# A decoder layer on one core: the projections moved one step further ahead of the scores, with their transfers in another order

## What is computed

```python
q, k, v = (split_heads(x @ W.T + b) for each of the three)
scores = (q @ Wq_lsr) @ (k @ Wk_lsr).T / sqrt(32)
attn = softmax(where(causal, scores, -inf))
x = layernorm(x + (attn @ v) @ Wo.T + bo)
x = layernorm(x + cross_attention(x, ctx))      # 120 context rows, 8 heads' width
x = layernorm(x + ffn(x, x shifted by one token))
```

## Time and profile before

| | us |
|---|---|
| median of 3 runs (lowest, highest) | 1104.71 (1097.24, 1111.92) |
| the profiled execution, its time | 1103.24 |
| its span, first to last instruction | 1101.5 |
| TensorE busy, share of the span | 980.6, 89% |
| DVE busy | 809.7, 74% |
| ACT busy | 582.0, 53% |
| POOL busy | 285.3, 26% |

### The profile page before, as it was taken

One profiled execution on the slowest core, in us unless ns is written; L12 is line 12 of the kernel. 1 busy time (PEld: TensorE's weight loads), 2 busy tenths in 40 slices (PEclk: granted clock), 3 DMA queues, 4 the chain that ended last, 5 costly groups with the idle time before them and its releaser, 6 DMA issues.

```text
span 1101.5 us, 24092 instructions
## 1 busy us (share of the span) xinstructions
PE 980.6 (89%) x8740; PEld 761.0 (69%) x8804; DVE 809.7 (74%) x1725; ACT 582.0 (53%) x1121; POOL 285.3 (26%) x537
## 2 busy tenths in 40 slices
PE   4667899999999999999999999999999999998863
PEld 4446677777777777777776777777777777776652
DVE  5335788788788787878787878878888787876453
ACT  1123455556665555566565555666555555565532
POOL 5000122222233222223322222223322223222332
PEclk9678999999999998999999999999999999999886
DMA  7664565666565566664655566655655666660000
GB/s 178 117 109 102 110 112 105 126 131 125 114 121 102 112 111 103 131 126 107 119 112 109 108 106 131 131 116 119 111 114 120 108 103 128 131 122 25 21 11 19
DMA packets 114784, 118.57 MB, mean 108 GB/s; under 512 B 20649, under 2 KB 98283, under 8 KB 114667
## 3 DMA queue, kind: packets, MB, share of 16 engines
q1 hardware_dynamic: 114667, 117.03, 54.4%
HBM read 74.00 MB, written 41.94 MB: 105 GB/s over the span
## 4 chain that ended last, share of the span: by engine, by line
DMA 38%; PE 26%; SPq 16%; ACT 8%; issue 7%; POOL 2%; DVE 2%; ACTq 0%; POOLq 0%; DVEq 0%
DMA parts_dram<-parts 25%; SPq L358 12%; DMA stack<-parts_dram 12%; PE ps_m L482 5%; PE ps_m L474 3%; PE ps_t L500 3%; PE ps_s L500 3%; ACT sum L703 2%; PE ps_t L506 2%; ACT x L679 2%; PE ps_o L552 2%; ACT yT_hi L696 1%; SPq L329 1%; PE ps_s L506 1%; ACT parts L671 1%
## 5 line engine op out<-in xcount | busy, mean ns | idle before, releaser
L662 ACT ACTIVATE p<-ps_t 128x1024 f32<-128x1024 f32 x192 | 196.6, 1024 | 129.3 <-PE ps_t L506 110.5
L856 DVE TENSOR_REDUCE row_max<-ps_s 128x4 f32<-128x1024 f32 (+1 forms) x192 | 232.8, 1213 | 43.2 <-PE ps_s L506 28.5
L1054 POOL TENSOR_TENSOR var<-mv,eps 128x2 f32<-128x2 f32 x96 | 18.8, 196 | 602.0 <-DVE mv L879 602.0
L500 PE MATMUL ps_s<-stack 48*128 48x128 f32 (+1 forms) x1024 | 109.3, 313 | 46.4 <-DMA stack<-parts_dram 41.3
L500 PEld LDWEIGHTS ps_s<-stack 48*128 48x128 f32 x1024 | 73.7, 191 | 82.4 <-DMA stack<-parts_dram 46.4
L500 PEld LDWEIGHTS ps_t<-stack 50*128 50x128 f32 x1024 | 73.7, 191 | 61.9 <-issue 43.3
L500 PE MATMUL ps_t<-stack 50*128 50x128 f32 (+1 forms) x1024 | 109.5, 314 | 5.3 <-ACT p L662 3.2
L772 ACT COPY kxT<-ps_m 128x240 f32<-128x240 f32 x32 | 11.5, 358 | 189.7 <-PE ps_m L454 189.7
L552 PE MATMUL ps_o<-p,v_pad 128*32 128x256 f32 (+1 forms) x2048 | 96.3, 329 | 0.0
L552 PEld LDWEIGHTS ps_o<-p,v_pad 128*32 128x32 f32 x2048 | 57.5, 109 | 39.3 <-issue 17.4
L1080 POOL TENSOR_TENSOR xr_lo<-dx,xr_hi 128x512 fp32r<-128x512 f32 x32 | 40.8, 1274 | 141.9 <-ACT xr_hi L736 141.9
(11 more groups left out here) (167 smaller groups left out, 2801.8 us busy)
## 6 DMA issues: line engine op xcount, KB each, us to landing
stack<-parts_dram SPq DMA_DIRECT2D x384, 128.0 KB, 4.4
parts_dram<-parts SPq DMA_DIRECT2D x64, 512.0 KB, 5.3
x_in<-in_x_turned SPq DMA_DIRECT2D x32, 256.0 KB, 2.9
x_res<-in_x SPq DMA_DIRECT2D x32, 256.0 KB, 3.2
out_x<-sum SPq DMA_DIRECT2D x64, 128.0 KB, 1.8
ctxT<-in_ctx_turned SPq DMA_DIRECT2D x32, 120.0 KB, 5.6
stack<-shift_parts SPq DMA_DIRECT2D x128, 8.0 KB
p<-in_Wq SPq DMA_DIRECT2D x1, 256.0 KB, 2.8
```

The costliest lines, as they stand in the source:

```text
L500: nc.tensor.matmul(o, left[b.slot][r0:r0 + rows_n, h // 2, rows_at:rows_at + P], right[b.slot][r0:r0 + rows_n, h // 2, col:col + width], s ...
L662: nc.scalar.activation(p[c][:], ps_t[:], ACT.Exp).then_inc(exp_done[c], 1)
L856: nc.vector.tensor_reduce(row_max[:, tile, :, j0:j0 + nj], ps_s[:].rearrange("p (g j w) -> p g j w", j=nj, g=2), AX_X, ALU.max) \
```

## The change

The stage numbers become 0, 2, 3, 4, 5: IN runs two steps ahead of SCORES, and the other stages keep their distances. There is one step more in all. In SP's step, the parts of q and of k are each written as soon as they are there, x_in of the next batch follows the k parts, and the twelve stack loads stand last, behind the shift rows. Before it overwrites a slot in DRAM, SP waits for the loads from it of three batches ago. POOL sets the ones rows of slot 0 where it set all three before, and the other two after the constants; SP waits for a semaphore of the slot instead of `consts_ready`. The engines' `on` becomes a dictionary.

```diff
-IN, SCORES, PROBS, CROSS, FFN = range(5)
+IN, SCORES, PROBS, CROSS, FFN = 0, 2, 3, 4, 5
...
-            def load_x(b):
-                wait(sp, v_["xT_lo"], b.n)
-                sp.dma_start(x_in[:], tokens(x_turned, b.n).rearrange("(k p) t -> p k t", p=P)).then_inc(x_loaded, 16)
+            def save_parts(b, s, ready):
+
+                if b.n >= RING:
+                    sp.wait_ge(stack_loaded[b.slot], Batch(b.n - RING, IN).dma_count(12))
+                sp.wait_ge(v_[ready], b.n + 1)
+                sp.dma_start(parts_dram[s][b.slot].rearrange("(a p) w t -> p a w t", p=P), parts[s][:].bitcast(F32)) \
+                    .then_inc(parts_saved[s][b.slot], 16)
+
+            def load_stack(b, s, which):
+
+                sp.wait_ge(parts_saved[s][b.slot], b.dma_count(1))
+                for g in range(2):
+                    for row, part in enumerate(which):
...
 
             def step(at):
-
-                if live(at, IN) and at > 0:
-                    load_x(Batch(at, IN))
-                at = at - 1
                 b = Batch(at, IN)
+                if live(at, IN):
+                    save_parts(b, 0, "q_lo")
+                if live(at - 1, FFN):
+                    c = Batch(at - 1, FFN)
+                    for j in range(NT):
+                        sp.wait_ge(x3_ready[j], c.n + 1)
+                        sp.dma_start(tokens(out, c.n)[j * P:(j + 1) * P, :], x3[:, j, :]).then_inc(out_saved, 16)
+                if live(at, IN):
+                    save_parts(b, 1, "k_lo")
+                if live(at + 1, IN):
+                    sp.wait_ge(v_["xT_lo"], b.n + 1)
+                    sp.dma_start(x_in[:], tokens(x_turned, b.n + 1).rearrange("(k p) t -> p k t", p=P)).then_inc(x_loaded, 16)
                 if live(at, PROBS):
                     c = Batch(at, PROBS)
                     wait(sp, v_["sum1_done"], c.n)
                     sp.dma_start(x_res[:], tokens(x, c.n).rearrange("(j p) c -> p j c", p=P)).then_inc(x_res_loaded, 16)
-                if live(at, IN):
-
-                    if b.n == 0:
-                        sp.wait_ge(consts_ready, 1)
-                    if b.n >= RING:
-                        before_it = Batch(at - 3, IN)
-                        sp.wait_ge(t_filled, before_it.chunks_done(T_ORDER, T_ORDER[-1]))
-
-                    for s, ready, which in ((0, "q_lo", (0, 0, 1)), (1, "k_lo", (0, 1, 0))):
...
                 if live(at, SCORES):
-
                     c = Batch(at, SCORES)
                     wait(sp, filled["f_vx"], c.n - 1)
...
+                if live(at, IN):
+                    if b.n >= RING:
+                        before_it = Batch(b.n - RING, IN)
+                        sp.wait_ge(t_filled, before_it.chunks_done(T_ORDER, T_ORDER[-1]))
+                    load_stack(b, 0, (0, 0, 1))
+                    if b.n < RING:
+                        sp.wait_ge(ones_ready[b.n], 2)
+                    load_stack(b, 1, (0, 1, 0))
...
-            for r in range(RING):
+            def ones_rows(r):
                 for h in range(2):
-
-                    link(g.memset(stack[1][r][64 * h + 32:64 * h + 64].bitcast(F32), 1.0))
+                    g.memset(stack[1][r][64 * h + 32:64 * h + 64].bitcast(F32), 1.0).then_inc(ones_ready[r], 1)
+                    pool.wait_ge(ones_ready[r], h + 1)
+
+            ones_rows(0)
...
             g.memset(x2T[:, :, 0:1], 0.0).then_inc(consts_ready, 1)
+            pool.wait_ge(consts_ready, 1)
+            for r in range(1, RING):
+                ones_rows(r)
```

More of the change, by code:

```diff
@@ L218, in decoder_layer @@
         consts_ready = sem("consts_ready")
+        ones_ready = [sem(f"ones_ready{r}") for r in range(RING)]
         consts_step = sem("consts_step")
@@ L515, in step @@
             def step(at):
-                A, Sb, Pb, X, F = (Batch(at, s) for s in range(5))
-                on = [live(at, s) for s in range(5)]
+                A, Sb, Pb, X, F = (Batch(at, s) for s in (IN, SCORES, PROBS, CROSS, FFN))
+                on = {s: live(at, s) for s in (IN, SCORES, PROBS, CROSS, FFN)}
                 def S(c):
```

6 lines of the change are left out of this document (4 added, 2 removed).

## The result

The change makes the kernel faster: median 1066.48 us (1066.0 to 1068.84, 4 runs) beside 1106.16 us of the kernel before on the same chip (1097.24 to 1111.92), a ratio of 0.965 with a 95% interval of 0.959 to 0.972. The forecast was 1068. The profiled execution has a span of 1064.3 us against 1101.5.

A forecast was written before the change was run, and what follows sets the result against it. The prediction saw TensorE held by waits for stack loads and the half clock after them. From 1103.24 us it took 26.2 for the main stretch and 8.6 for the start, tail and ones rows 0: 1068.4 us, range 1057 to 1086.

The forecast's parts named there:

- The main stretch: S(0) of batch 4 to S(0) of batch 31: 838.1 us for 27 steps before, forecast 811.9.
- the 19.4 us of S(0) waits: TensorE's 21 waits for stack loads between 150 and 995 us, claimed to vanish with 15 us of slack.
- the 1.9 of T(0): Three waits of T(0) in the steady steps, 1.9 us in all, claimed to vanish.
- rival A: In the steady steps the wait moves to z1 or T(0); 1088 us if all 19.4 us return; chance 0.16.
- The step of 30.01 us: Step from 900.52 to 930.53 before the change, no wait at its end; taken as the reachable step length.
- term (1): Steady steps from S(0) of batch 4 to batch 31: waits and half clock go, gain 26.2 us.
- the rows' 5.7 us: Time lost to 17 us at half clock in the steady steps, priced from one step where 6.8 us cost 2.3.
- The Trainium skill's rule: Alternative half-clock price for the steady steps: throttled time times one minus clock ratio, 8.5 us, making the total 1065.6.
- The start: Up to S(0) of batch 4, forecast at 145.4: early waits and half clock vanish, gain 8.6 us.
- The step without projections: Step of batch 30, now without projections: claimed 30.9 us, as batch 31's step took before, nothing won.
- The tail behind it: From S(0) of batch 31 to the end: same order on all engines, no stacks to load, difference 0.
- Rival C: In each step x_in comes late behind the burst; 1138 us at stack loads of 1.9 us; chance 0.05.

The follow-up runs named there:

- x_first: The change with the load of the next x moved back to the front of SP's step, ahead of the parts: 1065.81 us, repeated 1066.71 us.
- loads_doubled: The change with twelve more loads of 112 KB a step ahead of the stack loads, into rows nobody reads: 1130.34 us.

## Why the prediction was right

**The main stretch.** Removing the 19.4 us of S(0) waits, the 1.9 of T(0) and the half clock gave 781.0 us for 26 steps; measured 779.4. The yT_lo waits of z1, 10.2 us before, are 8.4 over the whole stretch, and T(0) has none for the shift rows, so rival A did not come. The step of 30.01 us whose end had no wait in the kernel before was the right yardstick.

**The half clock.** It vanished from the main stretch, as term (1) said. The length of the stretch does not settle its price: by the rows' 5.7 us the 26 steps are 781.0 us, and measured were 779.4. Single steps speak for the rows' price, about a third: in the step of batch 1, some 7 us more at half clock made 2.6 us, and in the step of batch 30 3.4 made 1.2 and 13.7 made 4.6, as 6.8 made 2.3 before. The Trainium skill's rule (TensorE: Matmul & The Clock Gate, Terms), half of the throttled time, doesn't fit in these places. Over the whole stretch it would give 778.4 us and lies as near as the rows do, and its 1065.6 for the total is nearer to the first median than 1068.4 and farther from the second.

**The start.** S(0) of batch 4 was forecast at 145.4 and came at 145.71 in one profile and 149.12 in the other. Inside it errors cancelled by luck. k_lo of batch 1 came at 37.6 and not 39.8: xT_lo ended at 31.1 for 32.4, and from there it took 6.5 us for 7.4, partly at full clock. So q of batch 2, which waited 6.70 us for x, began at 43.66 and not 45.7. From its end to shift_lo it then took 15.9 us for 14.55, and T(0) of batch 0 came at 66.58 where 66.8 stood, having waited 3.35 for the shift rows. From there to S(0) of batch 2 it was 23.2 us and by the prediction 21.9, and the step of batch 2 was 25.9 for 26.7. S(0) of batch 0 was put at 37.7 and came at 35.75, which moved nothing behind it. x_first shows that the late load of x was real and not free: without it the start is 6 us shorter in its first profile (139.62) and 5 in its second (140.85). The prediction counted the delay as hidden by the old waits, which is right against the kernel before, and did not name it as an avoidable loss.

**The step without projections** (batch 30) was put at 30.9, after the step of batch 31. It took 29.66 in this profile, 30.88 in the second and, in x_first's two, 34.25 and 29.67. What the prediction took for its length was its length with 3.4 us of half clock in it. The tail behind it, put at no difference, was 109.5 and 112.6 us in the two profiles, 109.3 before.

**Room.** The landing of the stacks was put at +44.5 of a step and came at +40.1 (455.66); S(0) of 475.46 was met with almost 20 us to spare, and x_in with more than 13, not 7. Rival C placed the tight spot at x_in. loads_doubled shows that the shift rows give way first, alone in the queue only as long as everything ahead of them has drained by +24.5, with x_in close behind. Its price, 70 us at loads of 1.9 us each, can't be held against the 36 us that the main stretch lost there, since the load was another.

**The range** of 1057 to 1086 holds all ten runs of the change, 1066.0 to 1075.3. That these fall into two groups, six up to 1068.8 and four from 1072.3, was not foreseen; the gap of 7.8 us between the spans of their profiles is larger than the forecast's error of 1.9 us in the first median and 4.0 in the second.

**What was not argued.** That nearly the whole gain of the main stretch, some 27 of 29 us, can be had in the old step, by moving the q parts ahead of the out stores: 1077.0 us, where the change has medians of 1066.5 and 1072.4. The prediction credited this gain to the further step and its slack; the step gives room, but the waits would have gone almost entirely without it. The rows for it were there (parts behind stores issued at 443.92). The view of waits names the transfer; only the order of the queue shows what held it.

## What to carry to other kernels

Before adding a pipeline step to hide a transfer, look at what stands ahead of it in its queue: here the q parts stood behind stores that waited for another stage, and moving them alone gave 21 us of the change's 29 to 40 (each against the kernel before of its own set). A further step and a new order can be worthless or ruinous apart and good together, because a step moves the release of a ring slot (T(5)) relative to the queue; redo the timetable for every wait in the queue, not only for the one that is to go. Put the transfer with the shortest time from ready to needed at the front, and measure room by loading the queue, since the trace shows slack for each transfer and not which one breaks first.

## What the runs showed of the hardware

- With more traffic some of SP's own issues got slower. Between 170 and 900 us the median issue of x_in took 0.47 us in the change and 1.45 in loads_doubled, that of ctx 0.54 and 1.57, at a DMA share of 0.63 and 1.03 over the main stretch. The median of a stack load stayed at 0.43 and that of a shift row at 0.64 in both. Twelve stack loads in a row took 5.6 to 7.5 us of SP within the change alone.
- Half clock cost about a third of its length in the full steps (2.3 us for 6.8, 2.6 for 7.0, 4.6 for 13.7), and whether it came in a step with short idle times differed from run to run: the step of batch 30 was 29.66, 30.88 and 34.25 us in three profiles whose waits in it sum to 2.7, 2.7 and 1.7 us and none of which is over 1.5. Why it fell there stays open. The two profiles of the change have 82 and 106 us at half clock in all; at a third, the 24 more are an estimated 8 us, as much as the 7.8 between them.
- Two executions whose 26 main steps take 779.42 and 779.50 us still differ by 7.8 us in all, and the medians of the same kernel in two sets by 5.9. With that, a difference under some 5 us needs both kernels in one set and more than five runs.
